# Layer 0 feed-forward: another order of the tile, and part of the last butterfly level on TensorE

## The reference

```python
def act_quant(x):                 # per token
    scale = 128 / clip(max|x|, 1e-5)
    return clip(round(x * scale), -128, 127) / scale
def fwht(x):                      # over the last dim, 1024
    h = 1
    while h < n:
        a, b = pairs of x at distance h
        x = (a + b, a - b); h *= 2
    return x / sqrt(n)
def bitlinear(x, w):   return act_quant(x) @ weight_quant(w).T
def h_bitlinear(x, w): return act_quant(fwht(x)) @ weight_quant(w).T
gate = bitlinear(x, w_gate); up = bitlinear(x, w_up)      # 256 -> 1024
return h_bitlinear(silu(gate) * up, w_down)               # 1024 -> 256
```

## Time and profile before

| what | value |
|---|---|
| median of three runs | 1587.7 us (1584.02 to 1590.56) |
| the profiled execution, its own time | 1582.08 us |
| its span, first to last instruction | 1580.3 us |
| busy: PE, DVE, ACT, POOL | 1356.6, 1048.1, 793.6, 633.8 us |
| mean granted TensorE clock | 0.93 |

### The profile page before, as it was taken

The page is one execution under the profiler, slowest core; times in us unless marked ns, Lnnn a source line. Parts: engine busy times, 40 slices in busy tenths (PEclk is TensorE's granted clock), DMA queues, the critical chain, the costliest instruction groups (busy, mean ns, idle before and its releaser), DMA issues. The chain is left out here.

```text
span 1580.3 us, 29321 instructions
## 1 busy us (share of the span) xinstructions
PE 1356.6 (86%) x7991; PEld 851.3 (54%) x7992; DVE 1048.1 (66%) x2409; ACT 793.6 (50%) x2354; POOL 633.8 (40%) x658
## 2 busy tenths in 40 slices
PE   6889996777689787999979999988995899969993
PEld 3555553455444353665455666564873666645662
DVE  5898986788569747223647888855344888863224
ACT  4667673576510045331108888822442888833330
POOL 3112420999577232771011111112545664214661
PEclk8999998899899789999989999967997999988997
DMA  5130001400100040896200000410552111412224
GB/s 185 49 113 23 19 12 63 155 0 0 37 17 0 9 157 11 250 296 202 67 26 23 27 22 22 168 52 27 146 143 77 52 50 33 173 55 64 83 83 167
DMA packets 96447, 124.80 MB, mean 79 GB/s; under 512 B 11117, under 2 KB 76464, under 8 KB 96112
## 3 DMA queue, kind: packets, MB, share of 16 engines
q1 hardware_dynamic: 85760, 95.80, 19.0%
q0 software_dynamic: 10608, 28.07, 6.2%
HBM read 91.31 MB, written 33.43 MB: 79 GB/s over the span
## 5 line engine op out<-in xcount | busy, mean ns | idle before, releaser
L717 ACT ACTIVATE l0a_prob<-l0a_ps_s,l0a_neg_max 128x128 f32<-128x128 f32 x512 | 137.6, 398 | 72.6 <-DVE l0a_neg_max L559 67.0
L717 ACT ACTIVATE l2a_prob<-l2a_ps_s,l2a_neg_max 128x128 f32<-128x128 f32 x512 | 138.4, 401 | 26.8 <-DVE l2a_neg_max L559 22.0
L1160 ACT ACTIVATE l3a_prob<-l3a_ps_s,l3a_neg_max 128x256 f32<-128x256 f32 x256 | 104.3, 481 | 33.5 <-DVE l3a_neg_max L1074 31.8
L219 POOL TENSOR_TENSOR ln_rstd<-ln_var_eps,minus_half 128x4 f32<-128x4 f32 (+1 forms) x14 | 23.1, 1656 | 240.4 <-POOLq L183 208.6
L559 DVE TENSOR_REDUCE l2a_neg_max<-l2a_ps_s 128x4 f32<-128x512 f32 x128 | 85.6, 683 | 19.4 <-PE l2a_ps_s L815 18.5
L502 POOL TENSOR_TENSOR l2a_k_head<-l2a_kT,head_of_row 128x512 f32<-128x512 f32 x32 | 33.1, 1053 | 157.8 <-DMA l2a_kT<-k_rows 157.8
L568 DVE COPY l0a_probT<-l0a_ps_t 128x512 f32<-128x512 f32 x128 | 84.5, 681 | 14.5 <-PE l0a_ps_t L827 14.4
L1074 DVE TENSOR_REDUCE l3a_neg_max<-l3a_ps_s 128x2 f32<-128x512 f32 x128 | 84.0, 679 | 12.9 <-PE l3a_ps_s L1211 12.0
L559 DVE TENSOR_REDUCE l0a_neg_max<-l0a_ps_s 128x4 f32<-128x512 f32 x128 | 85.3, 682 | 9.9 <-PE l0a_ps_s L815 9.1
L502 POOL TENSOR_TENSOR l0a_k_head<-l0a_kT,head_of_row 128x512 f32<-128x512 f32 x32 | 32.6, 1040 | 139.7 <-DMA l0a_kT<-k_rows 139.7
L1819 PE MATMUL l1a_ps_y<-l1a_kv,l1a_tap 128*128 128x512 f32 x192 | 84.1, 601 | 3.7 <-POOL l1a_kv L1791 3.7
(11 more groups left out here) (475 smaller groups left out, 3529.6 us busy)
## 6 DMA issues: line engine op xcount, KB each, us to landing
l1f_w_gu<-in_l1f_w_gu SPq DMA_DIRECT2D x32, 352.0 KB, 6.2
expert_results<-zeros SPq DMA_DIRECT2D x1, 8320.0 KB, 26.3
l1f_got<-expert_results SPq DMA_DIRECT2D x16, 512.0 KB, 4.4
expert_results<-l2f_y_sb SPq DMA_DIRECT2D x47, 128.0 KB, 1.7
l1f_w_d<-in_l1f_w_d SPq DMA_DIRECT2D x32, 176.0 KB
l2f_w_gu_all<-in_l2f_w_gu SPq DMA_DIRECT2D x1, 4096.0 KB, 13.9
l3f_w_gu_all<-in_l3f_w_gu SPq DMA_DIRECT2D x1, 4096.0 KB, 14.8
l3f_got<-expert_results SPq DMA_DIRECT2D x16, 256.0 KB, 5.1
```

The source lines that it names most:

```text
L717: last = act.activation(prob[4 * c + j][:, r * P:r * P + P], ps_s[j][:, r * P:r * P + P], ACT.Exp, bias=neg_max[:, j, r:r + 1])
L1160: last = act.activation(prob[4 * c + j][:, m * D:m * D + D], ps_s[j][:, m * D:m * D + D], ACT.Exp, bias=neg_max[:, j, m:m + 1])
```

## The change

- **Butterflies.** The order of the levels is now distance 512, 256, 128. prod and mixed lie side by side in one tile `levels`, so that one operation of the second level can write its differences to two places: blocks 2 and 3 to prod, as input of the last level, and blocks 6 and 7 straight to mixed. The last level handles only three of the four block pairs on POOL (two operations of 384 elements). The fourth, blocks 6 and 7, is left to `transform`: block 6 is multiplied by [H, H] and block 7 by [H, -H], 256 columns wide, accumulated in the same PSUM. `had` holds H, H and -H for this; it is loaded twice by one DMA, and ACT makes the negative.
- **Clip of x.** clip_x goes from DVE to ACT as a Relu of (MAGIC + 127) - xr, and copy_xqT turns it back as 127 minus that. a_rec has two buffers. The transposed x of tile 4 and later goes through ps_g and not ps_q; turn_xq waits for silu of the tile before instead of for copy_hqT.
- **Rounding.** round_h writes ps_f in place; `rounded` is gone, quantise_h reads ps_f, and transform(t) waits for hq_done(t-1) instead of round_done.
- **deq** is made by two operations of one column each.
- **Order.** PE: turn_mixed(t, 0), down(t-2), turn_mixed(t, 1), gate(t+3), transform(t, 0), turn_hq(t-1, 0), transform(t, 1), turn_hq(t-1, 1), up(t+3), turn_xq(t+4). ACT: copy_mixedT(t, 0), norm(t+5), copy_mixedT(t, 1), silu(t+3), copy_hqT(t-1, 0), round_x(t+4), clip_x(t+4), copy_hqT(t-1, 1), copy_xqT(t+4), round_h(t). DVE: gate_times_up(t+2), add_to_x(t-2), measure_x(t+4), scale_h(t), quantise_h(t). The steps ahead of tile 0 on PE are longer by turn_xq(3), gate(2) and up(2); at the end PE has down(14) and DVE has add_to_x(14) behind tile 15.

The diff, cut to its core:

```diff
-        sp.dma_start(core.had[:, :], core.dram["had"]).then_inc(core.had_in, 16)
+        sp.dma_start(core.had[:, 0:2, :], core.dram["had"].unsqueeze(1).broadcast_to([P, 2, P])).then_inc(core.had_in, 16)
...
-                    pool.wait_ge(mixT_put, t - 1)
-                for n, (src, dst) in enumerate(((prod[u], fly), (fly, prod[u]), (prod[u], mixed[u]))):
...
+                    pool.wait_ge(mixT_put, 2 * t - 2)
...
+                even, odd = pairs(prod[u], W4)
+                high, low = pairs(fly[:, :], W4)
+                pool.tensor_tensor(high, even, odd, ALU.add)
+                pool.tensor_tensor(low, even, odd, ALU.subtract)
+                pool.drain()
+                even, odd = pairs(fly[:, :], 2 * P)
+                pool.tensor_tensor(pairs(prod[u], 2 * P)[0], even, odd, ALU.add)
+                pool.tensor_tensor(levels[u][:, :].rearrange("p (n c) -> p n c", c=2 * P)[:, 1:8:6, :], even, odd, ALU.subtract)
+                pool.drain()
+                even, odd = pairs(prod[u][:, 0:6 * P], P)
+                high, low = pairs(mixed[u][:, 0:6 * P], P)
+                pool.tensor_tensor(high, even, odd, ALU.add)
+                pool.tensor_tensor(low, even, odd, ALU.subtract).then_inc(mixed_done, 1)
...
-                dve.tensor_scalar(deq[u][:, :], w_mean[:, 0:2], a_max[u][:, :], None, ALU.mult)\
-                   .then_inc(deq_done, 1)
...
+                for n in range(2):
+                    dve.tensor_scalar(deq[u][:, n:n + 1], w_mean[:, n:n + 1], a_max[u][:, :], None, ALU.mult)\
+                       .then_inc(deq_done, 1)
...
-                dve.tensor_scalar(hq[:, :], rounded[:, :], MAGIC, 127.0, ALU.subtract, ALU.min).then_inc(hq_done, 1)
+                dve.tensor_scalar(hq[:, :], ps_f[:, :], MAGIC, 127.0, ALU.subtract, ALU.min).then_inc(hq_done, 1)
...
+                act.activation(xq[:, :], xr[:, :], ACT.Relu, bias=clip_at[:, :], scale=-1.0).then_inc(xq_done, 1)
...
-                act.activation(rounded[:, :], ps_f[:, :], ACT.Identity, bias=magic[:, :], scale=b_rec[:, :])\
+                act.activation(ps_f[:, :], ps_f[:, :], ACT.Identity, bias=magic[:, :], scale=b_rec[:, :])\
...
-                        pe.wait_ge(round_done, t)
-                for c in range(half * NF // 2, (half + 1) * NF // 2):
-                    last = pe.matmul(ps_f[:, c * P:c * P + P], mixedT[:, c * P:c * P + P], had[:, :], start=True, stop=True)
+                        pe.wait_ge(hq_done, t)
+                for c in range(half * NF // 2, (half + 1) * NF // 2 - 2 * half):
+                    pe.matmul(ps_f[:, c * P:c * P + P], mixedT[:, c * P:c * P + P], had[:, 0, :], start=True, stop=True)
                 if half:
+                    for n in range(2):
+                        last = pe.matmul(ps_f[:, 6 * P:8 * P], mixedT[:, (6 + n) * P:(7 + n) * P],
+                                         had[:, n:n + 2, :].rearrange("p n c -> p (n c)"), start=(n == 0), stop=(n == 1))
...
             def tile(t, u):
-                for half in range(2):
-                    turn_mixed(t, u, half)
-                    if ahead(t, 2):
-                        gate_up(t + 2, u, half)
+                turn_mixed(t, u, 0)
+                if after(t, 2):
+                    down(t - 2)
+                turn_mixed(t, u, 1)
+                if ahead(t, 3):
+                    gate_up(t + 3, 1 - u, 0)
                 for half in range(2):
                     transform(t, half)
                     if after(t, 1):
                         turn_hq(t - 1, half)
                 if ahead(t, 3):
-                    turn_xq(t + 3, 1 - u)
-                if after(t, 1):
-                    down(t - 1)
...
+                    gate_up(t + 3, 1 - u, 1)
+                if ahead(t, 4):
+                    turn_xq(t + 4, u)
...
+            turn_xq(3, 1)
+            gate_up(2, 0, 0)
+            gate_up(2, 0, 1)
             over_long_pipe(pe, tile)
+            down(B - 2)
```

More of the change, by code:

```diff
@@ L1311, in hadamard_ffn @@
         xqT = [sb(f"xqT{u}", [P, KC, P], BF16) for u in range(2)]
-        a_max, a_rec = [sb(f"a_max{u}", [P, 1]) for u in range(2)], sb("a_rec", [P, 1])
+        a_max, a_rec = ([sb(f"{n}{u}", [P, 1]) for u in range(2)] for n in ("a_max", "a_rec"))
         deq = [sb(f"deq{u}", [P, 2]) for u in range(2)]
@@ L1329, in hadamard_ffn, with ps_xqT @@
         ps_hqT = ps_q[:, 0:D].bitcast(BF16)
-        ps_xqT = ps_q[:, 0:P].bitcast(BF16)
+        first_xqT, later_xqT = (ps[:, 0:P].bitcast(BF16) for ps in (ps_q, ps_g))
+        def ps_xqT(t):
+            return first_xqT if isinstance(t, int) and t < 4 else later_xqT
         ps_y = ps_q[:, D:2 * D]
@@ L1437, in _ @@
             measure_x(0, 0)
-            clip_x(0)
             dve.wait_ge(rstd_done, 2)
@@ L1448, in _ @@
             over_x_pipe(dve, tile)
+            add_to_x(B - 2, 0)
             finish_rows(dve, core, 0, B - 1)
@@ L1462, in round_x, with clip_x @@
                     act.wait_ge(xq_done, t)
-                act.activation(xr[:, :], xn[u][:, :], ACT.Identity, bias=magic[:, :], scale=a_rec[:, :])\
+                act.activation(xr[:, :], xn[u][:, :], ACT.Identity, bias=magic[:, :], scale=a_rec[u][:, :])\
                     .then_inc(x_rounded, 1)
+            def clip_x(t):
+                act.wait_ge(x_rounded, t + 1)
+                if after(t, 1):
+                    act.wait_ge(xqT_put, t)
+                act.activation(xq[:, :], xr[:, :], ACT.Relu, bias=clip_at[:, :], scale=-1.0).then_inc(xq_done, 1)
             def copy_xqT(t, u):
@@ L1499, in tile @@
                 copy_mixedT(t, 0)
+                if ahead(t, 5):
+                    norm(t + 5, 1 - u)
                 copy_mixedT(t, 1)
-                if ahead(t, 2):
-                    silu(t + 2, u)
+                if ahead(t, 3):
+                    silu(t + 3, 1 - u)
                 if after(t, 1):
                     copy_hqT(t - 1, 0)
-                    copy_hqT(t - 1, 1)
-                if ahead(t, 3):
-                    copy_xqT(t + 3, 1 - u)
-                round_h(t)
                 if ahead(t, 4):
                     round_x(t + 4, u)
-                if ahead(t, 5):
-                    norm(t + 5, 1 - u)
+                    clip_x(t + 4)
+                if after(t, 1):
+                    copy_hqT(t - 1, 1)
+                if ahead(t, 4):
+                    copy_xqT(t + 4, u)
+                round_h(t)
+            act.wait_ge(core.had_in, 16)
+            act.activation(had[:, 2, :], had[:, 0, :], ACT.Copy, scale=-1.0).then_inc(had_ready, 1)
             act.wait_ge(shift_done, 1)
@@ L1524, in _ @@
             round_x(2, 0)
+            clip_x(2)
             act.wait_ge(shift_done, 2)
@@ L1529, in _ @@
             round_x(3, 1)
+            clip_x(3)
             norm(4, 0)
+            copy_xqT(3, 1)
+            silu(2, 0)
             over_x_pipe(act, tile)
```

68 lines of the change are left out of this document (29 added, 39 removed).

## The result

The changed kernel took 1593.4 us in the median of 17 runs (1587.7 to 1604.9), the kernel before 1587.7 on the same chip; the ratio is 1.0032, 95% interval [1.0016, 1.0048], so 2.5 to 7.6 us are lost. The forecast was 1588.4, its range 1581.5 to 1594.0, its likeliest outcome within 0.5%, and that is what came. But it forecast +0.7 us and about +5 were measured, and the interval excludes +0.7. The question is where the other 4 us come from.

What follows compares the result with a forecast made beforehand. It took a ring of waits, 8.28 us a tile, as the bound, POOL's 8.1 just under. Fourteen tiles -3.5, ramp +3.3, end +1.0: net +0.7 us, set on the median 1588.4; range 1581.5 to 1594.

Steps and rivals of the forecast that it cites:

- ring of 8.28: Steady tile before: the chain of waits from transform to next transform takes 8.28 us, POOL's 8.1 just under it.
- Part 1, ACT order: Steady loop: x operations no longer stand between round_h and the mixedT copy; 0.98 us removed, ring 7.30.
- Part 2, the wide matmuls: Last pair on PE: two matmuls 256 wide add 0.43 us a tile, ring 7.73.
- Rival A: Wide matmuls cost nothing extra, so DVE's ring binds; -5.7 us, 1582.7; chance 0.12.
- Part 3, down two tiles back: quantise_h from PSUM takes 1.20 us, so PE waits 0.09 in turn_hq(t-1, 0); period 7.82.
- Parts 4 to 6: DVE free at 5.62, needed at 5.97; ACT has 0.1 to 0.2 to spare; POOL 7.1 to 7.7 us a tile.
- rival D: DVE's two 128x1 deq operations stay held by POOL; period 8.48, +7.9 us, 1596.3; chance 0.04.
- rival E: The Relu changes ACT's table, two loads a tile; ACT's queue 9.5 a tile, +21 us, 1610; chance 0.02.
- rival C: ACT's queue binds and round_h comes late; 8.2 us a tile, +4.6, 1593.0; chance 0.11.
- rival F: POOL keeps its clash with DVE; +0.3 us, counted inside the forecast's chance of 0.55.
- The ramp: First tiles: turn_xq(3), gate(2), up(2) delay transform(0) by 3.4 us; R(0), round_h(0)'s start on ACT, at 296.21.
- The end: After tile 15's rounding: quantise_h +0.53 and add_to_x(14) +0.48 us, adding 1.0.

Runs made afterwards that it cites:

- hq_sbuf: Changed kernel with rounding into an SBUF tile again, quantise_h reading from there, and the waits that go with it; stage 158.18 us, ratio 1.0037.
- pool_end_warm: Changed kernel with all four last-level pairs on POOL and ten unread matmuls on PE before the last half transposes; stage 148.35 us, ratio 0.9985.
- ramp_warm: Changed kernel with tile 3's x measured before tile 1's product, and unread matmuls in PE's gaps of first and last tiles; stage 148.36 us, ratio 0.9988.
- warm_pe: Changed kernel plus unread matmuls in PE's gaps in tile 1, tiles 13 to 15 and before the last half transposes; stage 153.79 us, ratio 1.0011.
- pair_on_pool: Changed kernel with all four block pairs of the last level on POOL again; stage 148.71 us, ratio 0.9991.

## Why the prediction was right or wrong

**The place and the bound.** A ring of 8.28 with POOL just under it was right: with the ring cut, POOL idles 0.67 us a tile. What the steady tile doesn't show is that POOL worked without a gap in the kernel before as well, from its second tile on, and was done 140.11 us after the stage's start, 0.06 ahead of turn_mixed(15, 0). Ring and POOL bounded that stage together.

**Part 1, ACT order.** Right: the copy of mixedT follows the rounding at once, 1.11 later.

**Part 2, the wide matmuls.** Right. Four instructions of 256 columns take 1.03 us in line (356.29). From the second half's start to b_max are 1.57 us (355.79 to 357.36) where 1.15 were: 0.42, taken 0.43. Undoing them takes only 0.37 off a tile, since DVE's ring is reached first, at 7.47 as forecast. Rival A is out.

**Part 3, down two tiles back.** Right. quantise_h took 1.225 us in every tile (taken: 1.20), turn_hq comes 4.18 us after the rounding and 4.08 in hq_sbuf, so the added wait is 0.10 (taken: 0.09). The rule of the Trainium skill, VectorE: DVE Perf Modes, section Why PSUM operands drop a tier, holds in this case: 1.225 us from PSUM, 0.695 from SBUF for the same 1024 elements.

**Parts 4 to 6.** Right. The 128x1 deq operations are never held: two in 0.32 us, so rival D is out. The Relu takes 0.51 us (forecast 0.59), copy_xqT 0.48 (0.48), and the only table load of the stage is at the first silu: rival E is out. ACT isn't late for round_h: rival C, as argued, is out too, though its time is where the result lies. POOL's fourth operation takes 1.27 for the 1.71 of the earlier trace rows, and the 384-wide ones 1.00 for 1.27; rival F is out. Two slips in the forecast's sums change nothing: rival A has DVE's ring at 7.49 where part 4 has 7.47, and rival D has DVE free at 6.63 where 5.62 and 0.99 are 6.61.

**The ramp.** The mechanism was right (PE waits 3.43 us ahead of turn_xq(3), and tile 0 stands behind it), the size too large. R(0) came 29.04 to 29.6 us after the start, not 30.2. The rows of after:

```profile
284.81 0.39 PE L1566 MATMUL l0f_ps_q<-identb,l0f_xq 128*128 128x128 bf16 x2 [3.43 <-ACT l0f_xq L1477]
...
286.70 1.49 PE L1577 MATMUL l0f_ps_u<-w_int,l0f_xqT 128*128 128x512 bf16 x4
288.03 0.60 PE L1588 MATMUL l0f_ps_t<-ident,l0f_levels 128*128 128x128 f32 x4
...
290.67 1.59 PE L1597 MATMUL l0f_ps_f<-had_matrix,l0f_mixedT 128*128 128x128 f32 x12
```

turn_xq(3) came at 284.81, 0.84 before the forecast's 285.65, since prod(1) came at 281.50 and not at 282.25. A part of that is the clip of tile 2: turn_xq(2) came 0.88 us earlier than before (278.02 for 278.90), where 0.6 was taken. Most of the rest is the clock in up(1), 1.47 us long where the same four matmuls took 1.91 before. up(2) took 1.33 us to the next row's start, not 1.7: there the clock rose before 288, where the step carried the half clock of the earlier trace rows to 289.25. Together transform(0) came 1.27 earlier than forecast, at 290.67 and not at 291.94. In pool_end_warm the clock was still 0.50 from 288 to 292, and there turn_mixed(0, 0) came 23.33 us after the stage's start, as the forecast had it (23.26).

**The end.** turn_hq(15, 0) came 2.97 us after R(15), forecast 2.96; the end +1.06, forecast +1.0 (0.97 in the table's figures). The last down took 1.89 us in both kernels, at half clock, and 1.05 in ramp_warm: a loss that both kernels share and that neither nor the forecast looked at.

**The step that failed** is one that the sum used without a word in each line behind the ramp: that PE keeps its full clock from R(0) to the end, since the earlier trace rows has 1.00. "R(1) has no add_to_x to wait for: 296.21 + 7.73" and "R(14) and R(15) have neither gate nor measure: 2 x 7.73" were both priced as what is no longer done. But what is no longer done there leaves PE idle. In tile 1, down's place between the two halves of turn_mixed is empty (idle 2.22 us before 296.77). Tiles 13 to 15 have no gate and up left, since these now come three tiles ahead and not two. The clock fell to half in both places, and the steps took 9.28 and 10.48 us for 7.73, which is +4.3. With the ramp's -1.2 that is 3.1 of the error of 3.4 us, and warm_pe shows the cause by taking both falls away. What makes the clock fall in one tile and hold in another with as long a gap stays open: pair_on_pool has the gap of 2.22 us without the fall.

The chances put 0.86 on what came, and the range held it. That was luck in part: nothing in the cases was a loss of 4 us by the clock, and the 1593.0 of rival C, which set the upper end, is another mechanism.

## What to carry to other kernels

When a step is moved some tiles ahead or back, look at the tiles at the two ends of the loop where its place is empty: price not only the work that is gone but the clock of the engine that now stands idle there, from narrow windows and not from one over the whole stage. The fall isn't certain, so price it as a case of its own, with a chance. Work moved to relieve an engine pays only when that engine comes to bind; first find out which of the others would be late next, and try the relief with and without it. An engine that works without a gap from its first piece to its last bounds the stage even where a shorter ring sets the pace for a while: ask when it starts and when it is done, and not only what it needs for one tile.
